# bf16 masks, onehot and class table on three rows a class, moments nine ahead until batch 5, and class sums ahead of the picks

## The reference

```
h   = max(layernorm(x, axis=-1), 0)
fv  = mean of h over the 256 rows, L2-normalised            # one value a node
idx = the 9 largest of fv_i * fv_j in each row i, first dropped
A   = 0/1 adjacency of idx, symmetric, diagonal 1           # 1024 x 1024
g   = relu((A / deg) @ (h.T @ W.T + b1))
out = x + ((A / deg) @ (g @ W.T + b2)).T
```

## Time and profile before

| | |
|---|---|
| median of 3 runs | 516.19 us (516.15 to 516.75) |
| profiled execution | 516.48 us, span 514.5 us |
| mean granted TensorE clock | 0.981 of 2.4 GHz |
| TensorE (PE) | 483.9 us busy |
| GpSimd (POOL) | 388.3 us |
| VectorE (DVE) | 359.8 us |
| ScalarE (ACT) | 349.6 us |
| weight loads (PEld, beside PE) | 331.1 us |
| DMA | 127.90 MB, mean 249 GB/s |

### The profile page before, as it was taken

The page is one execution under the profiler, slowest core; times in us unless marked ns, Lnnn a source line. Parts: engine busy times, 40 slices in busy tenths (PEclk is TensorE's granted clock), DMA queues, the critical chain, the costliest instruction groups (busy, mean ns, idle before and its releaser), DMA issues.

```text
span 514.5 us, 7304 instructions
## 1 busy us (share of the span) xinstructions
PE 483.9 (94%) x2338; PEld 331.1 (64%) x2338; DVE 359.8 (70%) x892; ACT 349.6 (68%) x723; POOL 388.3 (75%) x367
## 2 busy tenths in 40 slices
PE   1998996879999999999999999999999999999996
PEld 0256574555777667775777667766777667777774
DVE  5989885987876798668976797768874565433334
ACT  4767987527777777767777777767777755555551
POOL 0257645866988889897988798887898887887773
PEclk9998998879999999999999999999999999999999
DMA  8982258987999789896989798996887344444424
GB/s 308 370 354 83 82 172 315 298 214 292 325 318 315 229 264 348 298 331 224 335 313 321 236 301 281 346 311 206 313 255 241 103 173 165 163 164 163 164 82 164
DMA packets 34629, 127.90 MB, mean 249 GB/s; under 512 B 2848, under 2 KB 3360, under 8 KB 34592
## 3 DMA queue, kind: packets, MB, share of 16 engines
q1 hardware_dynamic: 30752, 113.82, 57.5%
q0 software_dynamic: 3840, 13.63, 14.7%
HBM read 68.72 MB, written 33.55 MB: 199 GB/s over the span
## 4 chain that ended last, share of the span: by engine, by line
PE 69%; DVE 12%; DMA 10%; ACT 4%; POOL 2%; issue 1%; SPq 1%; DVEq 0%; ACTq 0%; POOLq 0%
PE ps L677 37%; PE ps L683 19%; PE ps L707 4%; DMA out<-res 4%; DMA h_sum<-hb 3%; PE aux L642 3%; PE aux L738 3%; DMA xin<-x 2%; DVE res L991 2%; DVE fv L849 2%; DVE best L840 1%; DVE best L853 1%; DVE found L857 1%; ACT hb L364 1%; PE aux L624 1%
## 5 line engine op out<-in xcount | busy, mean ns | idle before, releaser
L535 POOL TENSOR_TENSOR r_lo<-r,r_hi 128x512 fp32r<-128x512 f32 x128 | 169.7, 1408 | 26.1 <-ACT r_hi L433 24.5
L524 POOL TENSOR_TENSOR h_lo<-hb,h_hi 128x512 fp32r<-128x512 f32 x128 | 171.3, 1401 | 7.4 <-ACT h_hi L396 7.3
L991 DVE SCALAR_TENSOR_TENSOR res<-ps,bias,res 128x512 f32<-128x512 f32 x128 | 90.0, 745 | 69.6 <-PE ps L714 69.5
L410 ACT ACTIVATE r<-ps,beta 128x504 f32<-128x504 f32 x64 | 43.7, 682 | 108.6 <-PE ps L707 93.4
L677 PE MATMUL ps<-r_hi,w_hi 128*128 128x512 f32 x256 | 109.1, 426 | 1.6 <-ACT r_hi L425 1.6
L677 PE MATMUL ps<-h_hi,w_hi 128*128 128x512 f32 x256 | 104.1, 407 | 2.5 <-DVE res L991 2.5
L677 PE MATMUL ps<-r_hi,w_lo 128*128 128x512 f32 x256 | 102.5, 400 | 0.0
L677 PE MATMUL ps<-h_hi,w_lo 128*128 128x512 f32 x256 | 102.2, 399 | 0.0
L364 ACT ACTIVATE hb<-xin,nmean,rstd 128x1024 f32<-128x1024 f32 x60 | 74.0, 1237 | 11.4 <-DVE nmean L833 7.3
L812 DVE BATCH_NORM_STATS2 stats<-xin 128x6 f32<-128x512 f32 x120 | 74.3, 677 | 9.7 <-DMA xin<-x 9.6
L683 PE MATMUL ps<-h_lo,w_hi 128*128 128x512 f32 x256 | 73.3, 408 | 0.0
(11 more groups left out here) (104 smaller groups left out, 583.3 us busy)
## 6 DMA issues: line engine op xcount, KB each, us to landing
res<-x SPq DMA_DIRECT2D x32, 1024.0 KB, 5.8
out<-res SPq DMA_DIRECT2D x31, 1024.0 KB, 4.2
xin<-x SPq DMA_DIRECT2D x28, 1024.0 KB, 8.3
h_sum<-hb SPq DMA_DIRECT2D x24, 512.0 KB, 4.2
h_sum<-hb POOLq DMA_DIRECT2D x24, 512.0 KB, 5.4
xin<-x SPq DMA_DIRECT2D x4, 512.0 KB, 5.2
h_sum<-x SPq DMA_DIRECT2D x2, 1024.0 KB, 9.9
out<-res SPq DMA_DIRECT2D x4, 256.0 KB, 2.3
```

The costliest lines, as they stand in the source:

```text
L410: nc.scalar.activation(r[:, m, K_TOP:H], bank[m][:, K_TOP:H], ACT.Relu, accum_out=src2[:, m, e, C_COMMON:C_COMMON + 1], **com)
L524: last = nc.gpsimd.tensor_tensor(h_lo[:, kf, n], hb[:, b % NH, kf, n], h_hi[:, kf, n].bitcast(F32), ALU.subtract)
L535: last = nc.gpsimd.tensor_tensor(r_lo[:, kf, n], r[:, kf, n], r_hi[:, kf, n].bitcast(F32), ALU.subtract)
L991: nc.vector.scalar_tensor_tensor(res[:, b % NR, m, n], bank[m][:], bias2[:, m:m + 1], res[:, b % NR, m, n], ALU.add, ALU.add).then_inc(out ...
```

## The change

1. `mask`, `onehot`, `v_hi` and `tab` are bfloat16, and a new `v_mid` with them. A class has three rows in place of two: 24 rows of a quadrant. `table` makes three parts in four steps (the rest lies in PSUM, `REST`), and `src3` is reduced in three copies.
2. TensorE's class product moves from between high and low products to between the two halves of the high product.
3. Moments run nine batches ahead until slot 5 and ten from there on; normalising, roots, copies and folds move with them. Batch 12's moments leave the slots of batches 1 and 2. In a group's last slot ScalarE normalises at the end, and the copy and the fold of that batch follow in the next slot.
4. In the slot in which the nine largest are sought, VectorE reduces the class sums before `top_rows`, `top_mark` moves behind the next table, and ScalarE's `zeros` behind the split of the second half.

Tiles and rows:

```
-        onehot = sb("onehot", [P, 2, 2, N], F32R)
+        onehot = sb("onehot", [P, 2, 2, N], BF16)
...
-        mask = sb("mask", [P, P], F32R)
+        mask = sb("mask", [P, P], BF16)
...
-        src3 = sb("src3", [P, KF, 2 * NCLS])
-        v_hi = sb("v_hi", [P, P], F32R)
-        tab = sb("tab", [P, P], F32R)
+        src3 = sb("src3", [P, KF, 3 * NCLS])
+        v_hi = sb("v_hi", [P, P], BF16)
+        v_mid = sb("v_mid", [P, P], BF16)
+        tab = sb("tab", [P, P], BF16)
...
+        REST = aux[:, P:2 * P]
...
             a = 32 * ((b % G + 2 * m) % G)
-            return slice(a, a + 2 * NCLS)
+            return slice(a, a + 3 * NCLS)
```

SyncE, slot t:

```
-                if t == 1:
-                    copy_h(LEAD)
-                    copy_h(LEAD + 1)
-                if t == 2:
-                    copy_h(LEAD + 2)
-                if 1 < t < NB - LEAD - 1:
-                    copy_h(t + LEAD + 1)
+                if t in (1, 2, 6):
+                    copy_h(t + LEAD - (t == 1))
+                    copy_h(t + LEAD + (t > 1))
+                elif t in (4, 5):
+                    copy_h(t + LEAD)
+                elif t > 6:
+                    if t % G == 0 and t + LEAD < NB:
+                        copy_h(t + LEAD)
+                    if t % G < G - 1 and t + LEAD + 1 < NB:
+                        copy_h(t + LEAD + 1)
```

ScalarE, slot t (`both(b)` normalises both blocks):

```
-                if t == 1:
-                    normalise(LEAD + 1, 0)
-                    normalise(LEAD + 1, 1)
+                if t in (1, 4, 5):
+                    both(t + LEAD)
...
+                if t == 6:
+                    root(t + LEAD + 1)
...
                     take_sums(group_at(t, 0))
-                    zeros(group_at(t, 0))
...
-                elif 1 < t < NB - LEAD - 1:
-                    normalise(t + LEAD + 1, 0)
-                    normalise(t + LEAD + 1, 1)
-                    if t == 2:
-                        root(LEAD + 4)
+                elif t == 5:
+                    root(t + LEAD + 1)
+                elif (t == 2 or t > 5 and t % G < G - 1) and t + LEAD + 1 < NB:
+                    both(t + LEAD + 1)
...
                 split_r(t + 1, 1)
+                if group_at(t, 0) is not None:
+                    zeros(group_at(t, 0))
...
-                elif 2 < t < NB - LEAD - 2:
-                    root(t + LEAD + 2)
+                elif t in (3, 4):
+                    root(t + LEAD + 1)
+                elif t == 5:
+                    both(t + LEAD + 1)
+                elif t > 5:
+                    if t + LEAD + 2 < NB:
+                        root(t + LEAD + 2)
+                    if t % G == G - 1 and t + LEAD + 1 < NB:
+                        both(t + LEAD + 1)
```

GpSimd, slot t:

```
-                elif 1 < t < NB - LEAD - 1:
-                    fold(t + LEAD + (t > 2))
+                elif t in (2, 4, 5):
+                    fold(t + LEAD)
+                elif t > 5 and t % G < G - 1 and t + LEAD + 1 < NB:
+                    if t == 6:
+                        fold(t + LEAD)
+                    fold(t + LEAD + 1)
...
+                if t > 6 and t % G == 0 and t + LEAD < NB:
+                    fold(t + LEAD)
```

TensorE, layer 1:

```
-                product_hi(bank, h_hi, n)
-                if between is not None:
-                    between()
+                product_hi(bank, h_hi, n, between=between)
```

VectorE:

```
             def table(b):
                 dve.wait_ge(v2_done, b + 1)
                 nc.vector.tensor_copy(v_hi[:], V2).then_inc(vhi_ready, 1)
-                dve.wait_ge(vhi_ready, b + 1)
-                nc.vector.scalar_tensor_tensor(tab[:], v_hi[:].bitcast(F32), c_("less"), V2,
-                                               ALU.mult, ALU.add).then_inc(tab_ready, 1)
+                dve.wait_ge(vhi_ready, 3 * b + 1)
+                nc.vector.scalar_tensor_tensor(REST, v_hi[:], c_("less"), V2, ALU.mult, ALU.add).then_inc(vhi_ready, 1)
+                dve.wait_ge(vhi_ready, 3 * b + 2)
+                nc.vector.tensor_copy(v_mid[:], REST).then_inc(vhi_ready, 1)
+                dve.wait_ge(vhi_ready, 3 * b + 3)
+                nc.vector.scalar_tensor_tensor(tab[:], v_mid[:], c_("less2"), REST, ALU.mult, ALU.add).then_inc(tab_ready, 1)
...
-                ahead = t + LEAD + 2
+                ahead = t + LEAD + (2 if t > 5 else 1)
...
+                if group_at(t - 1, 0) is not None:
+                    top_mark(group_at(t - 1, 0))
...
+                if t == 5:
+                    scales(t + LEAD + 1)
+                    spreads(t + LEAD + 2, 0)
                 if group_at(t, 0) is not None:
+                    class_terms(t + 1)
                     top_rows(group_at(t, 0))
```

41 lines of the change are left out of this document (22 added, 19 removed).

## The result

| | before | after |
|---|---|---|
| median | 516.47 us (4 runs beside it) | 532.12 us (4 runs, 529.04 to 537.00) |
| profiled execution, span | 516.48, 514.5 us | 531.76, 529.8 us |
| mean granted clock | 0.981 | 0.97 |

The ratio of the runs is 1.0249, with a 95% interval of 1.0131 to 1.0367: slower, though the interval leaves open whether by more than 2%. The forecast was 517.4, its range ended at 520.8.

What follows compares the result with a forecast made beforehand. TensorE, busy 94%, was taken as the bound, so only its work or waits count. Start +2.7, batches 5 to 7 +2.3, groups' first slots −1.4 and bf16 −2.4 gave +1.2 on 516.19: 517.4 us, range 512.8 to 520.8.

Steps and rivals of the forecast that it cites:

- Start: Batches 0 to 4: 0.7 us at batch 0's table plus 2.0 of half clock behind the sums, +2.7 us; bounds −3.9 to +4.
- landed 5.4 later as folds do in the median: Start, group 2's last fold: issued at 110.73, landing 5.4 us later at 116.16 as before, so column sums start at 116.9.
- transfers follow TensorE: Rival at the start: copies and folds come 3.9 us earlier, kept in place of 2.7 lost; 510.8 us, chance 0.05.
- Batches 5 to 7: Slots 5 to 7: 1.6 us waiting for group 3's last fold, 0.7 for table 7; +2.3 us, bounds 0 and 3.5.
- A group's first slot: Class sums reduced first, table still late: some 0.55 of 0.82 us waiting stays; 0.24 won five times, 0.2 once, −1.4 us.
- bf16, −2.4 forecast: Masks and terms products on TensorE: bare weight load of 0.11 us at 45 places, 0 to 5.0 us saved, middle taken.
- Rival 1: Tiled products of masks and terms lose their whole bare load, 0.11 us at 45 places: −1.4, 514.8 us; chance 0.29.
- up to four times: TensorE weight loads: Fast Weight Load, with 128 weights of a type other than FP32, is up to four times as fast.
- size is not what sets it: TensorE, tiled weight loads: a 16-row load's record is as long as a full one's; given as evidence against Rival 1.
- keeps some 0.25 us more slack: Plain slots: class product 0.93 us earlier against a table chain longer by 0.68, so the table has 0.25 us more slack.
- The late table in plain slots: Rival: VectorE's scales or third table step take 0.6 us more; some 20 slots wait 0.3 each, +7, 524 us; chance 0.07.
- Ten matmuls at 0.42 in place of 0.235: Start, behind TensorE's wait for `r_lo` near 93.2: half clock slows ten matmuls, costing +2.0 us.

Runs made afterwards that it cites:

- loads_behind_fold: Changed kernel with copies, normalising and folds as before from slot 7, batch 5's `res` load and the x load held until group 2's folds land: 517.9 us.
- old_order: Changed kernel with moments, normalising, copies and folds in the order of before; bf16, earlier class product and new group-slot order stay: 512.2 us, 0.992 of the kernel before.
- fp32r_new_places: Kernel before (fp32r, two rows, old copy order) with the earlier class product and new order in a group's first slot: 512.7 us, 0.991 of the kernel before.
- bf16_two_rows: fp32r_new_places with `onehot`, `mask`, `v_hi` and `tab` in bf16, still two rows a class: 506.9 us, again 508.8; 0.985 of the kernel before.
- loads_behind_both_groups: loads_behind_fold with slot 6's `res` load and the next `xin` load also held until group 3's folds land: 517.2 us, 1.000 of the kernel before.

## Why the prediction was wrong

**Start, +2.7 forecast, 7.0 measured.** The wait moved to `r_lo` (93.2, 94.00), the code's comparison at 1.2, the half clock behind both waits: right. At batch 0 the mechanism was right and the size was not. TensorE waits for the table 3.32 us, where I had 1.18 and 0.68 more, and behind it the clock is 0.50 (52.6 to 56.0), where it was 1.00 in the trace before (53 to 56; its half clock lay earlier, 0.54 in 47.7 to 51), and I had priced nothing. Batch 2's class product comes 2.4 us later, measured as above, about as much as two profiles of one kernel differ by there, and the wait for `r_lo` takes up most of it. The step that failed reads "landed 5.4 later as folds do in the median". It landed 9.6 later, because the part that I counted as won (batch 2 finished earlier) sends two loads of 1 MB out ahead of the fold. loads_behind_fold shows it: the same fold lands in 4.8. I had asked whether transfers follow TensorE and gave it 0.05 as a gain; the loads did follow, and that was the loss.

**Batches 5 to 7, +2.3 forecast.** The place was right, and that a fold lands too late there (the sums of group 3 stand 3.09; table 7 comes 0.36 late), the size was not: 1.6 us of waiting were 3.1, the half clock behind it was not priced, and `r_lo` costs 0.5 at 179.74. With bf16's gain taken out the slots lose about 5.3 (4.7 + 0.1 at six places). The upper bound of 3.5 was too low. Why the second of the two folds takes 7.7 us is open.

**The loop, no term at all.** "normalising, roots, copies and folds move with them" stood in the change, and I priced copies and folds of slots 7 to 22 at nothing without a sentence. It is the worst omission: 8 to 10 us. The copies' median landing rose from 4.2 to 8.7 us. I had the DMA share of two early stretches only the earlier trace rows and never looked at the loop's, which is 0.96.

**A group's first slot, −1.4 in six.** A group of four is 1.04 us shorter in old_order. With 0.76 of it bf16's, 0.28 is left for the slot, 1.4 in five. The number is right; it is the balance of 0.87 won by the places and 0.59 lost to the third row.

**bf16, −2.4 forecast.** Rival 1's mechanism is the true one: 0.1 us a place (0.423 to 0.314 us from terms to the next full load), the whole bare load. The Trainium skill (TensorE: Matmul & The Clock Gate, Weight-path perf modes) says that the fast load comes on by itself when the number of weights is 128 and their type is not FP32; its factor of four is the theory for fp8, for bf16 it tells of two elements read at a time, and it gives about two as measured. The trace agrees: 183 to 91 ns, a factor of two, so the prediction's "up to four times" was not bf16's figure. I took the middle for want of a row, and between a fifth and half of the gain was missed. The rule "size is not what sets it" held: 24 rows load in 90 ns, 16 fp32r rows in 183. bf16 needs the new place of the product, though, and my claim that a plain slot "keeps some 0.25 us more slack" was right only with both together: 0.56 against 0.34.

At 0.095 a place and the forecast's 45 places bf16 gives −4.3; by the ratios of fp32r_new_places and bf16_two_rows it is 0.6%, 3 us. With the slot's −1.4 and +0.7 at batch 0 the change without its new order should give −4 to −5; old_order has −4.2 by its ratio. All the rest is the new order of moments, copies and folds.

**Two sums.** The late table in plain slots was priced at +7 and 524 us; twenty slots of 0.3 are 6, which gives 523.4. Ten matmuls at 0.42 in place of 0.235 are 1.85 us, given as 2.0. Neither moves the forecast.

## What to carry to other kernels

Before a transfer is moved by one slot, list what else will be issued in the slot that it comes to, also what leaves earlier because an engine got faster. A high DMA share there (0.96 in this case) says that the engines are full, not who will wait: 0.96 stood both ahead of a wait of 2.89 us and in a kernel with no such wait. Where a copy came late, reordering the engine that waits for it only changed which wait was paid. A landing time depends on the traffic beside the transfer: it is no constant, even where the median looks like one. When a precision trade lengthens a chain, count the chain's slack slot by slot first, and move its start ahead in the same change.

## What the runs showed of the chip that I had not expected

A bf16 weight load of 16 or 24 rows takes 91 ns, an fp32r one of 16 rows 183, and the 0.1 us between them is bare at each place where the tiling changes. VectorE's two-input comparison takes 1204 to 1220 ns in all eight places of the changed kernel, where it took up to 8615: nothing was changed in the instruction, only when it runs. In all nine profiles in which group 1's comparison began while GpSimd was in its row of subtractions it took 7.9 to 8.6 us, and in the ten others 1.2; in the kernel before it ended at 99.73, GpSimd's first gap behind 91.11 is at 98.64. No run was made to isolate this. And a fold of 0.5 MB by GpSimd's queue landed in 4.8 to 10.5 us in the changed kernel: 9.6 beside two 1 MB loads; in loads_behind_both_groups one took 7.1 behind another fold with no load beside it.
